# Probabilities times values by plain fp32 matmuls in a windowed attention block

## The chip, the cores and the metric

One core of a Trainium2 chip. The metric is the device time of one execution in microseconds. Engines are named as the profile names them: PE is TensorE (PEld its weight loads), DVE VectorE, ACT ScalarE, POOL GpSimd, SP SyncE, which here issues the transfers.

## The reference

Input x of 8 batches, 512 rows, 256 columns. Three blocks follow each other:

- x = x + 0.5 * FFN(layernorm(x)), where the FFN is another layernorm with gamma and beta, one 256 x 256 product with the weight quantized to -1, 0, 1, and a bias;
- x = x + attention(layernorm(x)): 16 query heads and 4 key/value heads of 128, rotary embedding on q and k, a causal window of 64 keys back, softmax, weights @ v, and an output projection Wo with bias;
- the first block once more.

The changed part is this line of it, with v repeated for the 4 query heads of a group:

```python
weights = jax.nn.softmax(scores, axis=-1)
out = jnp.einsum('bhqk,bhkd->bhqd', weights, v)
```

## The kernel before, in words

A batch's attention is cut into 16 units: 4 groups (one key/value head and its 4 query heads) times 4 blocks of 128 rows, and a block into 2 chunks of 64 queries. A chunk of 64 queries sees a window of 128 keys. So there are 128 units in the 8 batches. A unit passes through these steps:

- S, `scores` (L576): 4 plain fp32 matmuls of 128 columns, onto a mask that ScalarE wrote into the bank;
- VectorE's negated maxima (L747), ScalarE's exponentials with row sums (L913), VectorE's reciprocals (L753), GpSimd's scaling (L1023);
- T, `transpose_probs` (L622): 4 transposes into the bank probsT_p;
- probsT leaves the bank in two parts. ScalarE copies it to an fp32r tile, the high part (`probsT_high`, L945); VectorE subtracts that from the bank, the low part (`probsT_low`, L766);
- W, `values` (L607): for each of the 2 chunks the helper `three` (L567) does high x high, high x low, low x high as fp32r matmuls, values as weights, probsT as the 256 moving columns;
- `heads_high` (L938) and `heads_low` (L758) take the result out in two parts, and O, `project` (L593), multiplies them by Wo: 4 x 3 fp32r matmuls of 256 columns.

Beside the units stand jobs that share two banks in turn: K and Q (projections with rotary products by VectorE, L771, a swap of halves by two transfers, L538, a sum by GpSimd, L1030), V (values, 4 a batch; ScalarE's high part L968, VectorE's low part L792), and the FFN's and layernorms' transposes and products. A job waits in `wait_for_bank` (L629) until the job two before it has left its bank. For V that is the low part, by the semaphore v_lo. Odd chunks' windows start in the middle of a block, so values are also kept shifted by 64 rows in v_odd, filled by transfers from v_s (`shift_values`, L525): for each half batch 4 transfers, two for the high part and two for the low. W of the first unit of each half batch waits for them (L614).

The order of the work is written out by hand: one table a queue (TENSOR, VECTOR, SCALAR, GPSIMD, SYNC, L58 to L207), each with a prologue, a first, middle and last batch and an epilogue. In a name such as probsT14p the letter p, c or n says the previous, current or next batch. TensorE's order interleaves units and jobs, as "O7c W8c T9c S11c", so that a unit's evacuations run beside other matmuls. No other queue than its own orders a step; between queues semaphores do. In TensorE's prologue V00n stands ahead of K0n Q0n Q1n Q2n Q3n V01n. The values' low part has its place on VectorE behind pieces of weight splits (w3i, w5i).

Plain fp32 matmuls stand in S, in the transposes, in the opening product with beta (`beta_product`, L709, 256 columns) and in the two that open the score banks (`open_banks`, L718, 512 columns).

Of the kernel before, what the change touches and what calls it, by code (L numbers as in the profile page):

```python
# [37 lines left out]
P = 128  # L38
# [58 lines left out]
        w4i XT0n w3i XT1n w5i V00n K0n Q0n Q1n Q2n Q3n V01n  # L97
    """,
    "first": """
        K1c Q4c max0c Q5c max1c inv0c Q6c inv1c w11f probsT0c max2c V10c Q7c max3c  # L100
        inv2c heads0c K2c probsT1c Q8c heads1c max4c inv3c stats0n probsT2c Q9c stats1n inv4c heads2c
        max5c V11c probsT3c inv5c Q10c heads3c probsT4c max6c Q11c heads4c w12f inv6c probsT5c K3c
        max7c YT0n heads5c Q12c probsT6c inv7c max8c YT1n heads6c Q13c probsT7c FO0n max9c inv8c
        astats0n Q14c heads7c FO1n inv9c astats1n probsT8c Q15c max10c heads8c probsT9c XT0n inv10c max11c
        XT1n heads9c probsT10c inv11c max12c K0n heads10c inv12c Q0n probsT11c max13c heads11c V00n Q1n
        max14c inv13c probsT12c Q2n heads12c max15c inv14c probsT13c Q3n V01n inv15c
    """,
    "middle": """
        heads13p probsT14p K1c Q4c evac0p heads14p stats0p max0c max1c probsT15p inv0c Q5c inv1c V10c
        heads15p Q6c max2c probsT0c Q7c evac1p inv2c stats1p heads0c YT0p probsT1c K2c max3c Q8c  # L110
        heads1c stats0n YT1p inv3c probsT2c Q9c max4c FO0p heads2c Q10c max5c inv4c probsT3c V11c
        heads3c inv5c max6c probsT4c FO1p Q11c inv6c stats1n heads4c max7c probsT5c K3c YT0n max8c
        heads5c probsT6c Q12c inv7c YT1n heads6c Q13c max9c inv8c FO0n probsT7c astats0n inv9c Q14c
        FO1n astats1n heads7c probsT8c max10c XT0n Q15c heads8c max11c probsT9c inv10c XT1n heads9c inv11c
        probsT10c K0n max12c Q0n max13c heads10c probsT11c inv12c V00n Q1n heads11c max14c inv13c probsT12c
        Q2n inv14c heads12c max15c inv15c probsT13c Q3n V01n
    """,
    "last": """
        heads13p K1c Q4c probsT14p evac0p max0c stats0p max1c heads14p inv0c probsT15p Q5c V10c Q6c
        inv1c heads15p probsT0c max2c Q7c evac1p stats1p inv2c heads0c max3c YT0p probsT1c K2c Q8c  # L120
        heads1c YT1p probsT2c max4c inv3c Q9c heads2c FO0p max5c probsT3c Q10c inv4c V11c heads3c
        inv5c probsT4c max6c FO1p Q11c heads4c probsT5c inv6c K3c max7c inv7c heads5c Q12c probsT6c
        max8c Q13c heads6c inv8c probsT7c max9c Q14c heads7c max10c probsT8c inv9c Q15c inv10c heads8c
        max11c probsT9c inv11c heads9c max12c probsT10c heads10c inv12c max13c probsT11c heads11c max14c inv13c probsT12c
        heads12c max15c inv14c probsT13c inv15c
    """,
    "epilogue": """
        heads13p probsT14p heads14p probsT15p evac0p stats0p heads15p evac1p stats1p YT0p YT1p FO0p FO1p
# [127 lines left out]
def unit(x):  # L256
    return UNITS * x[2] + x[1]


def block_kernel(nc, x, wq, wk, wv, wo, ffn_wT, columns, rows, rope_tables, mask, ident, out):  # L260
# [3 lines left out]
    with ExitStack() as ctx:  # L264
# [23 lines left out]
        v_s = sb("v_s", [P, 2, BLOCKS, NKV * HD], F32R)  # L288
        v_odd = sb("v_odd", [P, 2, BLOCKS - 1, NKV * HD], F32R)

        probs = sb("probs", [P, 2, 4, P])
        probsT = sb("probsT", [P, 2, 2, GROUP * CHUNK], F32R)
# [844 lines left out]
```

## Time and profile before

| what | value |
|---|---|
| runs | 810.41, 810.8, 811.8 us, median 810.8 |
| the profiled execution | 812.07 us, span 810.2 us |
| mean granted TensorE clock | 0.994 |
| ScalarE, GpSimd busy | 515.1, 449.9 us |
| transfers | 70.53 MB |

The span runs from the first to the last profiled instruction; some 2 us lie around it. "Busy" counts a stretch once if instructions overlap. Ends of matmuls are modelled, so two of them overlap in a list, and a group's mean duration is not the distance between two of them: for that, start times are compared. A plain fp32 matmul shows as two records. "x6" merges six records of one kind, and "[0.24 <-DVE headsT L762]" is idle time ahead of it and what ended it.

### The profile page before, as it was taken

Reading aid. Unit: us, or ns where it says so; the run is one execution under the profiler, and the core shown is the slowest. Engines: PE = TensorE matmul, PEld = TensorE weight load, DVE = VectorE, ACT = ScalarE, POOL = GpSimd, SP = SyncE. Lnnn points to the kernel's source line nnn. Section 1 sums busy time; section 2 is a strip of 40 time slices with the busy share of each in tenths; the row PEclk is TensorE's granted clock in tenths of the full one; section 3 lists DMA queues with packets and bytes.
Section 4 is the critical chain, followed back from the end, with each engine's and each line's share of the span. In section 5 each row is a group of like instructions: output and inputs, shape, how many; then the busy total and the mean of one; then the engine's idle time right before and its main releaser. Section 6 shows DMA issues by size and latency. Waiting matters only on the chain.

```text
span 810.2 us, 16063 instructions
## 1 busy us (share of the span) xinstructions
PE 787.2 (97%) x5678; PEld 734.2 (91%) x5678; DVE 640.0 (79%) x1294; ACT 515.1 (64%) x1633; POOL 449.9 (56%) x435
## 2 busy tenths in 40 slices
PE   7899999999999999999999999999999999999984
PEld 6689999999999999999999999999999999999984
DVE  5888868888788877888779786888878887787644
ACT  5377765676657665676656766567666666574662
POOL 4577736575465644566446664556546564464532
PEclk9999999999999999999999999999999999999997
DMA  8464224442342424323234332444234242424300
GB/s 296 117 159 96 50 53 106 103 99 45 67 119 66 110 49 105 91 66 92 53 91 104 89 71 53 105 104 98 44 74 113 66 112 47 104 53 105 79 2 26
DMA packets 52431, 70.53 MB, mean 87 GB/s; under 512 B 7040, under 2 KB 30080, under 8 KB 52352
## 3 DMA queue, kind: packets, MB, share of 16 engines
q1 hardware_dynamic: 52064, 69.43, 35.2%
q8 instruction: 45, 0.74, 0.4%
q14 instruction: 34, 0.28, 0.1%
q10 hardware_dynamic: 288, 0.08, 0.0%
HBM read 10.76 MB, written 4.19 MB: 18 GB/s over the span
## 4 chain that ended last, share of the span: by engine, by line
PE 86%; DVE 5%; ACT 2%; issue 2%; POOL 2%; DMA 2%; SPq 0%; ACTq 0%; POOLq 0%
PE job_p L572 29%; PE attn_p L572 22%; PE scores_p L588 12%; PE heads_p L572 11%; PE probsT_p L626 6%; PE job_p L698 4%; PE job_p L687 2%; ACT headsT L942 1%; DVE headsT L762 1%; DMA q_s<-wk 1%; ACT probs L920 1%; DVE parts L842 1%; POOL q_s L1046 1%; DVE variance L851 1%; DMA rope_swap<-rope_sin 1%
## 5 line engine op out<-in xcount | busy, mean ns | idle before, releaser
L1026 POOL TENSOR_TENSOR probs<-probs,inv_sum 128x512 f32<-128x512 f32 x128 | 134.4, 1050 | 197.5 <-DVE inv_sum L756 197.3
L920 ACT ACTIVATE probs<-scores_p,neg_max 128x128 f32<-128x128 f32 x512 | 181.0, 372 | 52.4 <-DVE neg_max L750 51.8
L572 PE MATMUL attn_p<-wo_s,headsT 128*128 128x256 f32 x1536 | 208.9, 285 | 5.3 <-DVE headsT L762 5.3
L572 PE MATMUL job_p<-xnT,wq_s 128*128 128x512 f32 x768 | 204.9, 403 | 1.9 <-DVE v_s L794 1.8
L572 PEld LDWEIGHTS attn_p<-wo_s,headsT 128*128 128x128 f32 x1536 | 195.5, 191 | 11.7 <-DVE headsT L762 7.3
L1046 POOL TENSOR_TENSOR q_s<-rope_cos,rope_swap 128x512 f32<-128x512 f32 x128 | 164.4, 1292 | 54.4 <-DMA rope_swap<-rope_sin 54.3
L942 ACT ACTIVATE headsT<-heads_p,columns_s 128x512 fp32r<-128x512 f32 x128 | 88.2, 689 | 154.3 <-PE heads_p L572 152.8
L572 PEld LDWEIGHTS job_p<-xnT,wq_s 128*128 128x128 f32 x768 | 135.9, 189 | 26.9 <-DVE v_s L794 2.7
L762 DVE SCALAR_TENSOR_TENSOR headsT<-heads_p,columns_s,headsT 128x512 fp32r<-128x512 f32 x128 | 95.7, 748 | 59.6 <-ACT headsT L942 58.2
L588 PE MATMUL scores_p<-k_s,q_s 128*128 128x128 f32 x1024 | 135.2, 275 | 0.4 <-POOL q_s L1046 0.4
L588 PEld LDWEIGHTS scores_p<-k_s,q_s 128*128 128x128 f32 x1024 | 125.8, 192 | 2.5 <-POOL q_s L1046 0.9
L784 DVE SCALAR_TENSOR_TENSOR rope_sin<-job_p,columns_s,rope_t 128x512 f32<-128x512 f32 x160 | 119.0, 744 | 8.7 <-PE job_p L572 7.4
L789 DVE SCALAR_TENSOR_TENSOR rope_cos<-job_p,columns_s,rope_t 128x512 f32<-128x512 f32 x160 | 118.7, 742 | 0.0
L920 ACT ACTIVATION_READ_ACCUMULATOR probs<-scores_p,neg_max 128x1 f32 x512 | 108.1, 211 | 0.0
L750 DVE TENSOR_REDUCE neg_max<-scores_p 128x4 f32<-128x512 f32 x128 | 86.8, 682 | 16.6 <-PE scores_p L588 16.4
L768 DVE TENSOR_TENSOR probsT<-probsT_p,probsT 128x512 fp32r<-128x512 f32 x128 | 86.6, 677 | 4.4 <-ACT probsT L948 4.4
L948 ACT ACTIVATE probsT<-probsT_p 128x512 fp32r<-128x512 f32 x128 | 76.4, 597 | 20.8 <-PE probsT_p L626 20.7
L572 PE MATMUL heads_p<-probsT,v_s 128*128 128x256 f32 x480 | 79.0, 284 | 0.0
L935 ACT ACTIVATE scores_p<-mask_s 128x512 f32<-128x512 bf16 x128 | 77.6, 607 | 0.7
L626 PE MATMUL probsT_p<-identf,probs 128*128 128x128 f32 x512 | 77.0, 273 | 0.4 <-POOL probs L1026 0.2
L1046 POOL TENSOR_TENSOR k_s<-rope_cos,rope_swap 128x512 f32<-128x512 f32 x32 | 41.4, 1293 | 49.1 <-DMA rope_swap<-rope_sin 49.1
L572 PEld LDWEIGHTS heads_p<-probsT,v_s 128*128 128x128 f32 x480 | 66.7, 191 | 0.5 <-DVE probsT L768 0.4
(73 smaller groups left out, 925.3 us busy)
## 6 DMA issues: line engine op xcount, KB each, us to landing
rope_swap<-rope_sin SPq DMA_DIRECT2D x320, 128.0 KB, 2.3
v_odd<-v_s SPq DMA_DIRECT2D x64, 192.0 KB, 3.3
x_in<-x SPq DMA_DIRECT2D x16, 256.0 KB, 3.3
out<-x_res SPq DMA_DIRECT2D x16, 256.0 KB, 2.5
staging<-wo SPq DMA_DIRECT2D x2, 512.0 KB, 10.5
staging<-wq SPq DMA_DIRECT2D x2, 512.0 KB, 10.7
x_res<-wo SPq DMA_DIRECT2D x2, 512.0 KB, 3.8
x_res<-wv SPq DMA_DIRECT2D x1, 512.0 KB, 7.3
```

What stands on the lines that cost most here:

```text
L572: mm = nc.tensor.matmul(dst, a(p), b(q), start=first and clears and i == 0, stop=last and i == 2, skip_group_check=True)
L588: mm = nc.tensor.matmul(dst[:, 2 * cc + pair, :], q_s[g % 2][:, c, 2 * pair:2 * pair + 2, :], k_s[:, g % 2, w0:w0 + P], start=False, stop= ...
L626: mm = nc.tensor.transpose(probsT_p[:, k, :], probs[:, x[1] % 2, k, :], identf[:, :])
L750: nc.vector.tensor_reduce(neg_max[:, i, :], scores_p[i][:, :, :], AX.X, ALU.max, negate=True).then_inc(max_ready, 1)
L762: nc.vector.scalar_tensor_tensor(out=flat_heads(headsT[:, 1]), in0=flat_heads(heads_p[:, :]), scalar=bv_s[:, g:g + 1], in1=flat_heads(head ...
L768: nc.vector.tensor_tensor(probsT[:, 1, :, :], probsT_p[:, :, :].rearrange("p (c a) n -> p c (a n)", c=2), probsT[:, 0, :, :].bitcast(F32), ...
L784: nc.vector.scalar_tensor_tensor(out=rope_sin[:, r, :], in0=bank[:, :], scalar=bias, in1=sin_t, op0=ALU.add, op1=ALU.mult).then_inc(rope_s ...
L789: nc.vector.scalar_tensor_tensor(out=rope_cos[:, r, :], in0=bank[:, :], scalar=bias, in1=cos_t, op0=ALU.add, op1=ALU.mult).then_inc(rope_c ...
L920: ins = nc.scalar.activation(probs[:, i, k, :], scores_p[i][:, k, :], ACT.Exp, bias=neg_max[:, i, k:k + 1], accum_out=row_sum[:, i, k:k + 1])
L942: nc.scalar.activation(flat_heads(headsT[:, 0]), flat_heads(heads_p[:, :]), ACT.Identity, bias=bv_s[:, g:g + 1]).then_inc(heads_hi, 1)
L1026: nc.gpsimd.tensor_tensor(probs[:, i, :, :], probs[:, i, :, :], inv_sum[:, i, :].unsqueeze(2).to_broadcast([P, 4, P]), ALU.mult).then_inc( ...
L1046: nc.gpsimd.tensor_tensor(roped(x), as_roped(x, rope_cos[:, r, :]), as_roped(x, rope_swap[:, r, :]), ALU.add).then_inc(rope_added, 1)
```

## The change

`values` does one plain fp32 matmul a chunk in place of three fp32r ones. v_s, v_odd and probsT become fp32 and have one part, which ScalarE writes as it wrote the high part. `probsT_low` and `values_low` are gone, and their places in VectorE's tables (128 and 32 steps). Banks and tiles are released by ScalarE's semaphores probsT_taken and v_taken, and a half batch is shifted by two transfers. The other queues' orders stay. The diff, with the tables cut to samples:

```diff
--- before.py
+++ after.py
@@ -94,38 +94,38 @@
     "prologue": """
         ones0i stats0n stats1n tern0i beta0i YT0n YT1n FO0n astats0n FO1n astats1n w2i w1i w0i
-        w4i XT0n w3i XT1n w5i V00n K0n Q0n Q1n Q2n Q3n V01n
+        w4i XT0n w3i XT1n w5i K0n Q0n Q1n Q2n Q3n 
     """,
...
     "middle": """
-        heads13p probsT14p K1c Q4c evac0p heads14p stats0p max0c max1c probsT15p inv0c Q5c inv1c V10c
-        heads15p Q6c max2c probsT0c Q7c evac1p inv2c stats1p heads0c YT0p probsT1c K2c max3c Q8c
...
+        heads13p K1c Q4c evac0p heads14p stats0p max0c max1c inv0c Q5c inv1c 
+        heads15p Q6c max2c Q7c evac1p inv2c stats1p heads0c YT0p K2c max3c Q8c
...
@@ -285,11 +285,11 @@
         q_s = [sb(f"q_s{i}", [P, SEQ // CHUNK, GROUP, CHUNK]) for i in range(2)]
         k_s = sb("k_s", [P, 2, SEQ])
         w_full = k_s[:, 0, :].rearrange("p (c n) -> p c n", c=EC)
-        v_s = sb("v_s", [P, 2, BLOCKS, NKV * HD], F32R)
-        v_odd = sb("v_odd", [P, 2, BLOCKS - 1, NKV * HD], F32R)
+        v_s = sb("v_s", [P, BLOCKS, NKV * HD])
+        v_odd = sb("v_odd", [P, BLOCKS - 1, NKV * HD])
 
         probs = sb("probs", [P, 2, 4, P])
-        probsT = sb("probsT", [P, 2, 2, GROUP * CHUNK], F32R)
+        probsT = sb("probsT", [P, 2, GROUP * CHUNK])
         headsT = sb("headsT", [P, 2, GROUP, 2, CHUNK], F32R)
         neg_max = sb("neg_max", [P, 2, 4])
         row_sum = sb("row_sum", [P, 2, 4])
@@ -358,8 +358,7 @@
         inv_ready = sem("inv_ready")
         probs_ready = sem("probs_ready")
         probsT_ready = sem("probsT_ready")
-        probsT_hi = sem("probsT_hi")
-        probsT_lo = sem("probsT_lo")
+        probsT_taken = sem("probsT_taken")
         heads_ready = sem("heads_ready")
         heads_hi = sem("heads_hi")
         heads_lo = sem("heads_lo")
@@ -371,8 +370,7 @@
         rope_cosed = sem("rope_cosed")
         rope_swapped = [sem(f"rope_swapped{i}") for i in range(ROPES)]
         rope_added = sem("rope_added")
-        v_hi = sem("v_hi")
-        v_lo = sem("v_lo")
+        v_taken = sem("v_taken")
         ln_hi = sem("ln_hi")
         ln_lo = sem("ln_lo")
         xn_hi = sem("xn_hi")
@@ -479,10 +477,10 @@
 
             return ("XT" if x[0][0] == "a" else "YT" + x[0][-1], *x[1:])
 
-        def v_part(i, s):
+        def v_part(i):
             half, m = i
             width = NKV * HD // 2
-            return v_s[:, s, 2 * m:2 * m + 2, half * width:(half + 1) * width]
+            return v_s[:, 2 * m:2 * m + 2, half * width:(half + 1) * width]
 
         def flat_heads(ap):
             return ap.rearrange("p h c q -> p (h c q)")
@@ -527,13 +525,10 @@
                 _, half, b = x
 
 
-                sp.wait_ge(v_lo, VALUES["V", (half, 1), b] + 1)
+                sp.wait_ge(v_taken, VALUES["V", (half, 1), b] + 1)
                 cols = slice(half * NKV * HD // 2, (half + 1) * NKV * HD // 2)
-                for s in range(2):
-                    sp.dma_start(v_odd[0:CHUNK, s, :, cols].bitcast(F32),
-                                 v_s[CHUNK:P, s, 0:BLOCKS - 1, cols].bitcast(F32)).then_inc(v_shifted, 16)
-                    sp.dma_start(v_odd[CHUNK:P, s, :, cols].bitcast(F32),
-                                 v_s[0:CHUNK, s, 1:BLOCKS, cols].bitcast(F32)).then_inc(v_shifted, 16)
+                sp.dma_start(v_odd[0:CHUNK, :, cols], v_s[CHUNK:P, 0:BLOCKS - 1, cols]).then_inc(v_shifted, 16)
+                sp.dma_start(v_odd[CHUNK:P, :, cols], v_s[0:CHUNK, 1:BLOCKS, cols]).then_inc(v_shifted, 16)
 
             def swap_halves(x):
 
@@ -608,15 +603,15 @@
                 u, (g, t), b = unit(x), divmod(x[1], BLOCKS), x[2]
 
 
-                pe.wait_ge(probsT_lo, u + 1)
+                pe.wait_ge(probsT_taken, u + 1)
                 if x[1] in (0, UNITS // 2):
 
-                    pe.wait_ge(v_shifted, 64 * (SHIFTED["shift", x[1] // (UNITS // 2), b] + 1))
+                    pe.wait_ge(v_shifted, 32 * (SHIFTED["shift", x[1] // (UNITS // 2), b] + 1))
                 for cc in range(2):
                     c = 2 * t + cc
                     src, at = (v_s, max(c - 1, 0) // 2) if c == 0 or c % 2 else (v_odd, c // 2 - 1)
-                    mm = three(heads_p[:, :, cc, :], lambda s: src[:, s, at, g * HD:(g + 1) * HD],
-                               lambda s: probsT[:, s, cc, :], True, True, cc == 0)
+                    mm = nc.tensor.matmul(heads_p[:, :, cc, :], src[:, at, g * HD:(g + 1) * HD], probsT[:, cc, :],
+                                          start=cc == 0, stop=True, skip_group_check=True)
                 mm.then_inc(heads_ready, 1)
 
             def transpose_probs(x):
@@ -634,7 +629,7 @@
                 if was[0] in ("Q", "K"):
                     pe.wait_ge(rope_cosed, ROPED[was] + 1)
                 elif was[0] == "V":
-                    pe.wait_ge(v_lo, VALUES[was] + 1)
+                    pe.wait_ge(v_taken, VALUES[was] + 1)
                 elif was[0] == "XT":
                     pe.wait_ge(xn_lo, XN[was] + 1)
                 elif was in FFN_IN:
@@ -763,11 +758,6 @@
                     out=flat_heads(headsT[:, 1]), in0=flat_heads(heads_p[:, :]), scalar=bv_s[:, g:g + 1],
                     in1=flat_heads(headsT[:, 0]).bitcast(F32), op0=ALU.add, op1=ALU.subtract).then_inc(heads_lo, 1)
 
-            def probsT_low(x):
-                dve.wait_ge(probsT_hi, unit(x) + 1)
-                nc.vector.tensor_tensor(probsT[:, 1, :, :], probsT_p[:, :, :].rearrange("p (c a) n -> p c (a n)", c=2),
-                                        probsT[:, 0, :, :].bitcast(F32), ALU.subtract).then_inc(probsT_lo, 1)
-
             def rope_products(x):
 
                 kind, i, b = x
@@ -788,11 +778,6 @@
                     dve.wait_ge(rope_added, n + 1 - ROPES)
                 nc.vector.scalar_tensor_tensor(out=rope_cos[:, r, :], in0=bank[:, :], scalar=bias, in1=cos_t,
                                                op0=ALU.add, op1=ALU.mult).then_inc(rope_cosed, 1)
-
-            def values_low(x):
-                dve.wait_ge(v_hi, VALUES[x] + 1)
-                nc.vector.tensor_tensor(v_part(x[1], 1), bank_of(x)[:, :].rearrange("p (k n) -> p k n", k=2),
-                                        v_part(x[1], 0).bitcast(F32), ALU.subtract).then_inc(v_lo, 1)
 
             def xn_low(x):
                 dve.wait_ge(xn_hi, XN[x] + 1)
@@ -891,8 +876,8 @@
                                                op0=ALU.mult, op1=ALU.add).then_inc(bias_ready, 1)
 
             for x in DVE_STEPS:
-                {"max": max_of, "inv": invert_sums, "heads": heads_low, "probsT": probsT_low,
-                 "K": rope_products, "Q": rope_products, "V": values_low, "XT": xn_low,
+                {"max": max_of, "inv": invert_sums, "heads": heads_low,
+                 "K": rope_products, "Q": rope_products, "XT": xn_low,
                  "YT1": ffn_in_low, "YT2": ffn_in_low, "FO1": ffn_out, "FO2": ffn_out,
                  "stats1": statistics, "stats2": statistics, "astats": statistics,
                  "evac": after_attention, "w": split_low, "ones": set_ones, "tern": ternary, "beta": fold_beta}[x[0]](x)
@@ -942,11 +927,11 @@
                 nc.scalar.activation(flat_heads(headsT[:, 0]), flat_heads(heads_p[:, :]), ACT.Identity,
                                      bias=bv_s[:, g:g + 1]).then_inc(heads_hi, 1)
 
-            def probsT_high(x):
+            def take_probsT(x):
 
                 act.wait_ge(probsT_ready, unit(x) + 1)
-                nc.scalar.activation(probsT[:, 0, :, :], probsT_p[:, :, :].rearrange("p (c a) n -> p c (a n)", c=2),
-                                     ACT.Copy).then_inc(probsT_hi, 1)
+                nc.scalar.activation(probsT[:, :, :], probsT_p[:, :, :].rearrange("p (c a) n -> p c (a n)", c=2),
+                                     ACT.Copy).then_inc(probsT_taken, 1)
 
             def normalize(x):
 
@@ -971,8 +956,8 @@
                 if b:
 
                     act.wait_ge(heads_ready, UNITS * (b - 1) + (UNITS if half else UNITS // 2))
-                nc.scalar.activation(v_part(x[1], 0), bank_of(x)[:, :].rearrange("p (k n) -> p k n", k=2),
-                                     ACT.Copy).then_inc(v_hi, 1)
+                nc.scalar.activation(v_part(x[1]), bank_of(x)[:, :].rearrange("p (k n) -> p k n", k=2),
+                                     ACT.Copy).then_inc(v_taken, 1)
 
             def xn_high(x):
                 act.wait_ge(job_ready, JOBS[x] + 1)
@@ -995,7 +980,7 @@
             act.wait_ge(power_ready, 1)
             nc.scalar.activation(thr[:, 3:4], minus_half[:, 0:1], ACT.Copy)
             for x in ACT_STEPS:
-                {"exp": exp_of, "mask": mask_bank, "heads": heads_high, "probsT": probsT_high,
+                {"exp": exp_of, "mask": mask_bank, "heads": heads_high, "probsT": take_probsT,
                  "norm1": normalize, "norm2": normalize, "anorm": normalize, "V": values_high, "XT": xn_high,
                  "YT1": ffn_in_high, "YT2": ffn_in_high, "w": split_high, "abs": sum_magnitudes}[x[0]](x)
```

## Rows read from the trace of the kernel before

**Rows 1.** The page, part 1: busy us (share of the span) xinstructions

```profile
PE 787.2 (97%) x5678; PEld 734.2 (91%) x5678; DVE 640.0 (79%) x1294; ACT 515.1 (64%) x1633; POOL 449.9 (56%) x435
```

**Rows 2.** Stretches: start:end length, busy us (x) of PE PEld DVE ACT POOL, clock, DMA

```profile
0.00:50.00 50.00, 40.46 (x217) 32.74 (x218) 37.50 (x74) 24.62 (x59) 27.71 (x29) 1.00 0.68 200
50.00:768.00 718.00, 716.72 (x5246) 673.63 (x5245) 582.94 (x1179) 469.73 (x1511) 408.51 (x394) 1.00 0.35 84
768.00:810.20 42.20, 30.02 (x218) 27.81 (x218) 19.61 (x44) 20.77 (x65) 13.64 (x14) 0.89 0.04 13
```

**Rows 3.** PE's waits, one row each of 50 to 768, 0 to 50, 768 on

```profile
PE attn_p L572 <- DVE headsT L762: 0.5, 2, 0.2
...
PE job_p L572 <- DVE v_s L794: 1.8, 1, 1.8
...
PE attn_p L572 <- DVE headsT L762: 5.0, 8, 1.6
```

**Rows 4.** Groups of instructions: shapes xcount | busy us, mean ns | idle before, releasers

```profile
L572 PE MATMUL heads_p<-probsT,v_s 128*128 128x256 f32 x480 | 79.0, 284 | 0.0
...
L572 PE MATMUL heads_p<-probsT,v_odd 128*128 128x256 f32 x288 | 50.3, 283 | 0.0
...
L572 PEld LDWEIGHTS heads_p<-probsT,v_s 128*128 128x128 f32 x480 | 66.7, 191 | 0.5 <-DVE probsT L768 0.4
...
L768 DVE TENSOR_TENSOR probsT<-probsT_p,probsT 128x512 fp32r<-128x512 f32 x128 | 86.6, 677 | 4.4 <-ACT probsT L948 4.4
...
L948 ACT ACTIVATE probsT<-probsT_p 128x512 fp32r<-128x512 f32 x128 | 76.4, 597 | 20.8 <-PE probsT_p L626 20.7
```

**Rows 5.** Timeline, PE, mid span: start us, us, what, xcount (merged)

```profile
405.28 0.88 PE L572 MATMUL heads_p<-probsT,v_s 128*128 128x256 f32 x6
406.00 0.60 PE L626 MATMUL probsT_p<-identf,probs 128*128 128x128 f32 x4
406.44 1.06 PE L588 MATMUL scores_p<-k_s,q_s 128*128 128x128 f32 x8
407.25 1.64 PE L572 MATMUL job_p<-xnT,wq_s 128*128 128x512 f32 x6
408.72 1.60 PE L572 MATMUL job_p<-wv_s,xnT 128*128 128x256 f32 x12
```

**Rows 6.** Timeline, PE, opening: transposes, beta product, opening of the score banks

```profile
7.73 1.11 PE L687 MATMUL job_p<-identf,y 128*128 128x128 f32 x4
8.64 1.06 PE L730 MATMUL heads_p<-identf 128*128 128x128 f32 x4
...
10.13 1.49 PE L714 MATMUL attn_p<-w_tern,columns_s 128*128 128x256 f32 x3
11.41 0.42 PE L687 MATMUL job_p<-identf,y 128*128 128x128 f32 x1
...
15.61 1.88 PE L723 MATMUL scores_p<-identf 128*128 128x512 f32 x4
17.32 1.05 PE L730 MATMUL heads_p<-identf 128*128 128x128 f32 x8
```

**Rows 7.** Timeline, all engines, 23 to 41 us: values and rotary sums

```profile
23.78 0.59 ACT L974 ACTIVATE v_s<-job_p 128x512 fp32r<-128x512 f32 x1
...
27.09 0.68 DVE L794 TENSOR_TENSOR v_s<-job_p,v_s 128x512 fp32r<-128x512 f32 x1
...
27.82 6.21 PE L572 MATMUL job_p<-xnT,wq_s 128*128 128x512 f32 x24 [1.76 <-DVE v_s L794]
...
36.41 3.80 POOL L1046 TENSOR_TENSOR q_s<-rope_cos,rope_swap 128x512 f32<-128x512 f32 x3 [1.87 <-DMA rope_swap<-rope_sin]
```

**Rows 8.** Timeline, PE, ending: one turn of the loop

```profile
781.41 0.88 PE L572 MATMUL heads_p<-probsT,v_s 128*128 128x256 f32 x6
...
783.86 1.70 PE L572 MATMUL attn_p<-wo_s,headsT 128*128 128x256 f32 x12 [0.24 <-DVE headsT L762]
...
785.39 0.52 PE L572 MATMUL heads_p<-probsT,v_odd 128*128 128x256 f32 x3
```

More of the change, by code:

```diff
@@ L103 @@
[L103 to L106, printed above, removed]
+        K1c Q4c max0c Q5c max1c inv0c Q6c inv1c w11f max2c Q7c max3c
+        inv2c heads0c K2c Q8c heads1c max4c inv3c stats0n Q9c stats1n inv4c heads2c
@@ L107 @@
+        max5c inv5c Q10c heads3c max6c Q11c heads4c w12f inv6c K3c
+        max7c YT0n heads5c Q12c inv7c max8c YT1n heads6c Q13c FO0n max9c inv8c
+        astats0n Q14c heads7c FO1n inv9c astats1n Q15c max10c heads8c XT0n inv10c max11c
+        XT1n heads9c inv11c max12c K0n heads10c inv12c Q0n max13c heads11c Q1n
+        max14c inv13c Q2n heads12c max15c inv14c Q3n inv15c
     """,
     "middle": """
-        heads13p probsT14p K1c Q4c evac0p heads14p stats0p max0c max1c probsT15p inv0c Q5c inv1c V10c
@@ L110 @@
-        heads15p Q6c max2c probsT0c Q7c evac1p inv2c stats1p heads0c YT0p probsT1c K2c max3c Q8c
[L111 to L114, printed above, removed]
@@ L115 @@
-        probsT10c K0n max12c Q0n max13c heads10c probsT11c inv12c V00n Q1n heads11c max14c inv13c probsT12c
-        Q2n inv14c heads12c max15c inv15c probsT13c Q3n V01n
+        heads13p K1c Q4c evac0p heads14p stats0p max0c max1c inv0c Q5c inv1c
+        heads15p Q6c max2c Q7c evac1p inv2c stats1p heads0c YT0p K2c max3c Q8c
+        heads1c stats0n YT1p inv3c Q9c max4c FO0p heads2c Q10c max5c inv4c
+        heads3c inv5c max6c FO1p Q11c inv6c stats1n heads4c max7c K3c YT0n max8c
+        heads5c Q12c inv7c YT1n heads6c Q13c max9c inv8c FO0n astats0n inv9c Q14c
@@ L117 @@
+        FO1n astats1n heads7c max10c XT0n Q15c heads8c max11c inv10c XT1n heads9c inv11c
+        K0n max12c Q0n max13c heads10c inv12c Q1n heads11c max14c inv13c
+        Q2n inv14c heads12c max15c inv15c Q3n
     """,
     "last": """
-        heads13p K1c Q4c probsT14p evac0p max0c stats0p max1c heads14p inv0c probsT15p Q5c V10c Q6c
-        inv1c heads15p probsT0c max2c Q7c evac1p stats1p inv2c heads0c max3c YT0p probsT1c K2c Q8c
-        heads1c YT1p probsT2c max4c inv3c Q9c heads2c FO0p max5c probsT3c Q10c inv4c V11c heads3c
@@ L122 @@
[L122 to L125, printed above, removed]
+        heads13p K1c Q4c evac0p max0c stats0p max1c heads14p inv0c Q5c Q6c
+        inv1c heads15p max2c Q7c evac1p stats1p inv2c heads0c max3c YT0p K2c Q8c
@@ L126 @@
+        heads1c YT1p max4c inv3c Q9c heads2c FO0p max5c Q10c inv4c heads3c
+        inv5c max6c FO1p Q11c heads4c inv6c K3c max7c inv7c heads5c Q12c
+        max8c Q13c heads6c inv8c max9c Q14c heads7c max10c inv9c Q15c inv10c heads8c
+        max11c inv11c heads9c max12c heads10c inv12c max13c heads11c max14c inv13c
+        heads12c max15c inv14c inv15c
     """,
     "epilogue": """
-        heads13p probsT14p heads14p probsT15p evac0p stats0p heads15p evac1p stats1p YT0p YT1p FO0p FO1p
+        heads13p heads14p evac0p stats0p heads15p evac1p stats1p YT0p YT1p FO0p FO1p
```

3 lines of the change are left out of this document (removed).

## The prediction

> **What bounds the kernel now.** I read the busy shares first. TensorE's matmuls are busy for 787.2 of 810.2 us, VectorE for 640.0, ScalarE for 515.1 [rows 1]. An average can hide stages, so the table of three stretches comes next [rows 2]: between 50 and 768 us matmuls are busy for 716.72 of 718.00 us, while VectorE has 135 us free. Before 50 us TensorE is busy for 40.46 of 50 us, behind 768 us for 30.02 of 42.20 us. Third, TensorE's own waits: in the 718 us the largest one, for headsT from VectorE, is 0.5 us in total; the opening has one of 1.8 us on VectorE's low part of the values; the ending has 5.0 us on headsT [rows 3]. So for 718 us the time is the sum of TensorE's own instructions. A removed VectorE instruction is worth nothing there, and a changed matmul is worth its full change. Only the two ends are chains of latencies.
>
> **Pace, not duration.** A matmul's listed duration (284 ns for heads_p [rows 4]) overlaps its neighbours', so I take paces from start times [rows 5]. Six matmuls of a unit's values start at 405.28 and the next step at 406.00: 0.72 us, 120 ns for one 256-column fp32r matmul. The scores are plain fp32 already: 512 matmuls leave 1024 records, two for one. Eight records of 128 columns start at 406.44, the next step at 407.25. That is 101 ns for each of eight, or 116 ns if the first matmul of the next step is only listed early and seven gaps make up the time. I take 112 ns, nearer the upper end, because the next step, the query projection, does look stretched: 1.47 us for six fp32r matmuls of 512 columns, 245 ns each, over twice 120. A transpose of 128 columns, also plain fp32, paces at 110 ns (0.44 us for four).
>
> **Part 1: values by plain fp32.** For each of 128 units two products of 256 columns replace 3 x 2 fp32r matmuls. Two records each makes four. What does one cost at 256 columns? The trace has three neighbours [rows 6]. At 512 columns, the four records that open the score banks start at 15.61 and the next step at 17.32: 427.5 ns each. At 128 columns it is 112 ns. A line through both gives 217.5 ns at 256. The third has the very shape: the product with beta, three records from 10.13 to 11.41, 427 ns each. But that is in the opening, where four transposes take 0.91 us (7.73 to 8.64) against 0.44 us later, so TensorE was at its 1.2 GHz level there although the granted clock is listed as 1.00 for the stretch. Halved, 213.5 ns. I take 216 ns, between them, with ends 213 and 218. A unit then takes 4 x 0.216 = 0.864 us in place of 0.72, 0.144 more, and **128 units 18.4 us more** (0.132 x 128 = 16.9 at the low end, 0.152 x 128 = 19.5 at the high end). Nothing hides it: in the middle TensorE has no idle time to give, and in the ending the values stand in the chain. There values start at 781.41, the projection waits for their evacuation until 783.86, and the next values start at 785.39 [rows 8], a loop of 3.98 us that holds the whole product once, so it too grows by 0.144 us a unit. Weight loads fall from six to four per unit; I credit them with nothing, because they run beside the matmuls.
>
> That the four records cost more than the six is the row's statement. The Trainium skill (FP8 and Floating Point Precision, TensorE Precision Notes) says that true fp32 takes four passes through the array. The paces agree in kind: two records of two passes each. They do not agree if every pass is charged at fp32r's 120 ns; that is a rival below.
>
> **Part 2: VectorE's low parts go.** 128 of probsT at 677 ns (86.6 us [rows 4]) and 32 of the values at 0.68 us (the one at 27.09 [rows 7]), 21.8 us. VectorE falls to about 532 us. In the middle this is worth at most the waits that exist: 0.5 us on headsT and some tenths on others. I take 0.5 us, ends 0 and 1.1 (718.00 less 716.72 with the rounding off). The probabilities become ready one VectorE step earlier, and no unit of the middle waits for them. Everything behind the removed steps on VectorE's queue (maxima, head low parts, rotary products) comes no later. Nothing new becomes late.
>
> **Part 3: releases by ScalarE.** The copies of probsT and values stay, one each, with an fp32 target where it was fp32r. No row has a copy to fp32. The nearest is the copy of probsT as it is, 597 ns [rows 4]; I take that. It could be somewhat shorter or as long as the 677 ns of VectorE's step beside it; both ends are covered, since that step of 677 ns no longer stands behind it on the way to TensorE. A bank of values is free after ScalarE's copy. This shows once: in the prologue ScalarE's copy starts at 23.78, the low part sits behind weight splits on VectorE until 27.09, and the query projection starts at 27.82 after a wait [rows 3, 7]. With the bank free at about 24.4 it can start when the key projection ends, at about 25.8: 1.9 us sooner. But the next three projections wait for rotary products on VectorE, which move up only by the 0.68 us removed there and a few tenths of better overlap; behind them come the swap transfers and GpSimd's sums, three in a row from 36.41 to 40.21, on which the first scores wait. So of 1.9 us **I take 1.1 us** as reaching the first scores, ends 0 (if the swap transfers land when they do now, next to the weight loads) and 1.9.
>
> **Part 4: the shift transfers.** Two in place of four for each half batch, half the bytes. SP's queue gets shorter ahead of the swaps of rotary products. No TensorE wait in the middle names them; credited at nothing. They can only make transfers earlier.
>
> **Sum.** +18.4 - 0.5 - 1.1 = **+16.8 us**. The profiled execution took 812.07 us around its span of 810.2; with the change 828.9. The median of the runs shown is 810.8, 1.3 below that execution, so the forecast is 827.6 us. Bounds: 16.9 - 1.1 - 1.9 = +13.9 (824.7) and +19.5 (830.3); with 1 to 2 us on each side for the seams between fp32r and fp32 steps and for the measurement, 823 to 832.
>
> **Rivals.**
> *Weight loads set the pace (ends faster).* TensorE's weight loads are busy for 91% of the span, and for values one takes 191 ns, longer than the 120 ns pace of its matmul [rows 1, 4, 5]. If each load, and not its columns, costs 120 ns, four loads take 0.48 us, 0.24 us less per unit: -30.7 us, and with the 1.6 us of gains 778.5. It decides if one record of 256 fp32 columns paces below 180 ns, the break-even 0.72/4. Against it: fp32 records pace at 112 with 128 columns and at 427.5 with 512 [rows 5, 6]; columns set it, not loads. Chance 0.03. The Trainium skill (Perfetto Trace Analysis, Identifying the Most-Contended Engine) would have TensorE judged by the busy share of weight loads and not by that of matmuls; by that, fewer loads should help, and the rows here speak against it.
>
> *Four passes at fp32r's pace.* If a pass costs what an fp32r matmul costs, a unit takes 8 x 120 = 0.96 us, 0.24 more: +30.7 - 1.6, 839.9 us. Against it: at 512 columns four passes take 2 x 427.5 = 855 ns, 214 a pass, under the 245 of one fp32r matmul [rows 5, 6]. Chance 0.04.
>
> *VectorE was what held TensorE.* If hidden delays by VectorE (79% busy) are in the middle's paces, 108 us less on it could pay for the matmuls. All idle time of TensorE in the span is 23.0 us [rows 1]; to break even 80% of it would have to vanish, and 12.2 us of it lie in the ending behind latencies that the change leaves alone. Even half of it gives 18.4 - 11.5, 817.7 us. Chance of 818 to 823: 0.04; of no change or better by it 0.02.
>
> *The change doesn't do what it says* (fp32 tiles still multiplied in one pass). Two matmuls of 120 ns a unit would show; -61 us. The scores' double records speak against. Chance 0.01.
>
> **How the numbers follow.** Forecast with its bounds: 0.86. A measurement of this kernel can tell about 0.2%, 1.6 us. Faster by more: 0.03 + 0.01 + 0.01 = 0.05; within: 0.01; slower: 0.94. The range 823 to 832 leaves out the rivals, 0.14 in all.
>
> **What the changed profile would show.** 512 records of heads_p with 256 columns where 768 stood; four of them and then the next step after 0.86 us (right) or 0.48 or 0.96 (rivals). Batches of the middle 2.3 us longer, 16 x 0.144. VectorE near 532 us busy. The wait on v_s gone and the first scores near 39.2 us. The ending's loop at 4.12 us for 3.98. I am wrong if the middle doesn't grow by some 16 us, or if a new wait of TensorE of more than 1 us stands in it.

## The result, and the profile after

The changed kernel takes **825.93 us** (median of 4 runs, 825.58 to 826.44), the kernel before 811.12 us beside it; the ratio is 1.0183, 95% interval 1.0166 to 1.0201. It is slower by 14.8 us, where +16.8 was forecast. The profiled execution took 826.44 us around a span of 824.6 us, 14.4 us more than the span of before.

The busy shares of the page, to be read against [rows 1]:

```profile
PE 803.1 (97%) x5422; PEld 733.7 (89%) x5422; DVE 547.3 (66%) x1134; ACT 516.0 (63%) x1633; POOL 448.9 (54%) x435
```

VectorE is 92.7 us less busy and TensorE 15.9 us more. (The removed VectorE steps summed to 108.4 us; busy time counts overlapping neighbours once, so it falls by less.) The stretches, against [rows 2], with the same columns:

```profile
0.00:50.00 50.00, 41.28 (x216) 34.24 (x217) 35.77 (x70) 25.09 (x61) 27.63 (x29) 1.00 0.65 192
50.00:780.00 730.00, 730.00 (x4993) 671.19 (x4992) 495.26 (x1026) 468.71 (x1506) 406.01 (x392) 1.00 0.32 74
780.00:824.60 44.60, 31.84 (x217) 28.27 (x215) 16.29 (x38) 22.25 (x67) 15.26 (x15) 0.96 0.06 18
```

For 730 us matmuls leave no gap that the profile shows. VectorE has 235 us free there, and no use for them. The groups of the changed instructions, against [rows 4] (out<-in shapes xcount | busy us, mean ns | idle before):

```profile
L613 PE MATMUL heads_p<-probsT,v_s 128*128 128x256 f32 x320 | 89.9, 378 | 0.0
...
L613 PE MATMUL heads_p<-probsT,v_odd 128*128 128x256 f32 x192 | 57.2, 379 | 0.0
```

320 and 192 make the 512 records, for 768. What they cost is in TensorE's timeline of the middle, against [rows 5]:

```profile
411.95 1.03 PE L613 MATMUL heads_p<-probsT,v_s 128*128 128x256 f32 x4
412.82 0.60 PE L621 MATMUL probsT_p<-identf,probs 128*128 128x128 f32 x4
413.25 1.06 PE L583 MATMUL scores_p<-k_s,q_s 128*128 128x128 f32 x8
414.07 1.63 PE L567 MATMUL job_p<-xnT,wq_s 128*128 128x512 f32 x6
```

Four records from 411.95 to 412.82 take 0.87 us (another unit: 406.93 to 407.80). In the five batches from 205 to 700 us a unit ahead of transposes takes 0.86 or 0.87 us, in the mean 0.866, so the forecast 0.864 holds. The steps beside it have kept their length: 0.43 or 0.44 us for the transposes, 0.82 or 0.81 for the scores.

A whole batch of the middle can be read off the chain of waits, where one merged piece of 18 matmuls returns once a batch. Before (start us, us, what):

```profile
203.54 2.81 PE job_p L572 x18
...
300.01 2.81 PE job_p L572 x18
...
396.31 2.82 PE job_p L572 x18
...
492.67 2.82 PE job_p L572 x18
...
588.65 2.82 PE job_p L572 x18
```

and after:

```profile
206.63 2.81 PE job_p L567 x18
...
304.75 2.81 PE job_p L567 x18
...
402.85 2.81 PE job_p L567 x18
...
500.97 2.81 PE job_p L567 x18
...
599.09 2.81 PE job_p L567 x18
```

Before, the batches take 96.47, 96.30, 96.36 and 95.98 us; after, 98.12, 98.10, 98.12 and 98.12. They have become longer, and even. Sixteen units at +0.145 would be +2.3; against the uneven batches of before only 1.6 to 2.1 shows. Something of 0.2 to 0.7 us a batch came back, though the largest wait of TensorE in that stretch of before was 0.5 us in all [rows 3].

The opening and the ending come from TensorE's waits (engine line waited for: us in total, times, longest; the first line is of 0 to 50 us, the second of 780 us on). The wait of 1.8 us on the values' low part [rows 3] is gone, and one of 1.1 us for a rotary product stands in its place; the ending's waits are as long as before:

```profile
PE job_p L567 <- DVE rope_cos L779: 1.1, 1, 1.1
...
PE attn_p L567 <- DVE headsT L757: 5.0, 8, 1.6
```

TensorE's timeline of the opening (the key projection, the query projections, the first scores), before and after; the query projections of before are in [rows 7]:

```profile
24.43 1.63 PE L572 MATMUL job_p<-xnT,wk_s 128*128 128x512 f32 x6 [0.69 <-DVE xnT L799]
...
40.27 2.05 PE L588 MATMUL scores_p<-k_s,q_s 128*128 128x128 f32 x16
```

```profile
25.32 1.61 PE L567 MATMUL job_p<-xnT,wk_s 128*128 128x512 f32 x6 [0.70 <-DVE xnT L784]
26.77 1.52 PE L567 MATMUL job_p<-xnT,wq_s 128*128 128x512 f32 x6
29.43 4.82 PE L567 MATMUL job_p<-xnT,wq_s 128*128 128x512 f32 x18 [1.14 <-DVE rope_cos L779]
...
40.40 1.95 PE L583 MATMUL scores_p<-k_s,q_s 128*128 128x128 f32 x16
```

and of the ending, against [rows 8]:

```profile
794.17 1.69 PE L567 MATMUL attn_p<-wo_s,headsT 128*128 128x256 f32 x12 [0.24 <-DVE headsT L757]
...
798.30 1.69 PE L567 MATMUL attn_p<-wo_s,headsT 128*128 128x256 f32 x12 [0.24 <-DVE headsT L757]
```

The first query projection now follows the key projection at 26.77; the next ones wait for rotary products, as foreseen. From the first key projection to the first scores it is 15.08 us (25.32 to 40.40). Before it was 15.84 us (24.43, the key projection, to 40.27). The scores' absolute time is no measure: in this execution the key projection itself starts 0.89 us later. The identity and the first part of x landed earlier than before, but the second part of x later (the statistics that wait for it start at 7.27 us, before at 6.62), and the FFN product behind it ends later. The changed steps have no part in that. The ending's loop takes 4.13 us, 794.17 to 798.30, for 3.98.

### The profile page after: what moved, and what is told of

Same layout as the page of the kernel before. It is cut to its first block, busy times and chain, and to the rows that moved or that the text cites. A ratio compares the mean times of both kernels' runs of the same rounds, so it can differ in the third digit from the quotient of the medians.

```text
span 824.6 us, 15359 instructions
## 1 busy us (share of the span) xinstructions
PE 803.1 (97%) x5422; PEld 733.7 (89%) x5422; DVE 547.3 (66%) x1134; ACT 516.0 (63%) x1633; POOL 448.9 (54%) x435
## 4 chain that ended last, share of the span: by engine, by line
PE 93%; DVE 3%; issue 1%; POOL 1%; ACT 1%; DMA 1%; SPq 0%; ACTq 0%; POOLq 0%
PE job_p L567 31%; PE attn_p L567 23%; PE heads_p L613 13%; PE scores_p L583 13%; PE probsT_p L621 6%; PE job_p L693 4%; PE job_p L682 2%; DVE headsT L757 1%; ACT headsT L927 1%; DMA x_in<-x 1%; POOL q_s L1031 1%; DVE parts L827 0%; DVE wq_s L740 0%; POOL wo_s L994 0%; PE attn_p L709 0%
## 5 line engine op out<-in xcount | busy, mean ns | idle before, releaser
L933 ACT ACTIVATE probsT<-probsT_p 128x512 f32<-128x512 f32 x128 | 76.3, 596 | 22.1 <-PE probsT_p L621 22.0
L613 PE MATMUL heads_p<-probsT,v_s 128*128 128x256 f32 x320 | 89.9, 378 | 0.0
L621 PEld LDWEIGHTS probsT_p<-identf,probs 128*128 128x128 f32 x512 | 63.3, 140 | 12.7 <-POOL probs L1011 0.5
L613 PEld LDWEIGHTS heads_p<-probsT,v_s 128*128 128x128 f32 x320 | 58.2, 189 | 7.2
```

Source lines behind the costliest of these rows:

```text
L613: mm = nc.tensor.matmul(heads_p[:, :, cc, :], src[:, at, g * HD:(g + 1) * HD], probsT[:, cc, :], start=cc == 0, stop=True, skip_group_chec ...
L621: mm = nc.tensor.transpose(probsT_p[:, k, :], probs[:, x[1] % 2, k, :], identf[:, :])
```

## The experiments

Two theories stood for the 4.1 us that came back (128 x 0.145 = 18.5 less the span's 14.4): VectorE's lighter queue, or the longer matmuls themselves, which cover small waits. A third, that the execution profiled before was an unlucky one, is taken up in the account further down. The first four kernels take the change apart.

**The matmuls alone.**

```diff
-                    mm = three(heads_p[:, :, cc, :], lambda s: src[:, s, at, g * HD:(g + 1) * HD],
-                               lambda s: probsT[:, s, cc, :], True, True, cc == 0)
+                    mm = nc.tensor.matmul(heads_p[:, :, cc, :], src[:, 0, at, g * HD:(g + 1) * HD].bitcast(F32),
+                                          probsT[:, 0, cc, :].bitcast(F32),
+                                          start=cc == 0, stop=True, skip_group_check=True)
```

> The kernel before with the matmuls of the values alone changed: plain fp32, on the high parts of values and probabilities; all of VectorE's low parts, their waits and transfers stay (the low parts are computed and not used, so the output lacks them). Pace theory: a unit's values take 0.865 us for 0.72, so 128 units cost 18.5 us. The changed kernel's span grew by only 14.4, so 4.1 us came back. If lighter VectorE queues gave them back, nothing comes back here: about 811.1 + 18.5 = 829.6 us. If the longer matmuls themselves cover small waits of TensorE in the middle (0.15 us at each batch's first key projection and some of 0.3 to 0.6), 3 us of it come back here too: about 826.5 us.

Measured: 827.65 us (826.97 to 828.26), ratio 1.0203, interval 1.0189 to 1.0217; before beside it 811.04. That is +16.6, between the two theories: 1.9 of the 18.5 came back with all of VectorE's work in place. Its batches, in the chain of waits:

```profile
305.61 2.81 PE job_p L572 x18
...
501.90 2.81 PE job_p L572 x18
...
600.37 2.81 PE job_p L572 x18
```

Two batches take 196.29 us, 98.15 each, and the third 98.47: near the whole change's 98.12, not quite as even. Its opening is that of before, 24.98 to 40.85, 15.87 us.

**No low parts, the matmuls as before.** From VectorE's tables all probsT and V steps go, a half batch is shifted by two transfers in place of four (the wait for v_shifted with them), and:

```diff
-                pe.wait_ge(probsT_lo, u + 1)
+                pe.wait_ge(probsT_hi, u + 1)
-                    mm = three(heads_p[:, :, cc, :], lambda s: src[:, s, at, g * HD:(g + 1) * HD],
-                               lambda s: probsT[:, s, cc, :], True, True, cc == 0)
+                    mm = three(heads_p[:, :, cc, :], lambda s: src[:, 0, at, g * HD:(g + 1) * HD],
+                               lambda s: probsT[:, 0, cc, :], True, True, cc == 0)
-                    pe.wait_ge(v_lo, VALUES[was] + 1)
+                    pe.wait_ge(v_hi, VALUES[was] + 1)
```

> The kernel before with three fp32r matmuls a chunk, but without VectorE's low parts of probabilities and values, the banks and tiles released by ScalarE, two shift transfers for four. All three matmuls read the high parts, so the low parts are left out of the result; TensorE's instructions are as many and as long as before. If the lighter VectorE gave the 4.1 us back: about 807 us. If the longer matmuls covered the waits: only the opening's 0.8 us, about 810.3 us.

Measured: 808.86 us, ratio 0.997 (0.996 to 0.9981), -2.2 us, again between the two theories. Taking 160 instructions, 108 us of work, from VectorE is worth 2.2 us. The parts add up: +16.6 - 2.2 = +14.4, the whole change +14.8. The opening is 24.92 to 40.03, 15.11 us. The batches:

```profile
298.67 2.82 PE job_p L565 x18
...
490.61 2.82 PE job_p L565 x18
...
586.57 2.82 PE job_p L565 x18
```

Two batches take 191.94 us, 95.97 each, and the third 95.96. So 95.97 is the batch with fp32r matmuls when no irregular wait is left, and the 96.30 to 96.47 of before held 0.3 to 0.5 us of such waits. But 98.12 less 95.97 is 2.15, not 2.32. One wait of 0.15 a batch is left in the kernel without low parts and absent after. It is at the key projection for the next batch. First before, then after:

```profile
291.33 0.52 PE L572 MATMUL heads_p<-probsT,v_odd 128*128 128x256 f32 x3
291.36 0.69 DVE L799 TENSOR_TENSOR xnT<-job_p,xnT 128x512 fp32r<-128x512 f32 x1 [0.31 <-ACT xnT L979]
...
291.69 0.52 PE L572 MATMUL heads_p<-probsT,v_s 128*128 128x256 f32 x3
...
292.19 1.17 PE L572 MATMUL job_p<-xnT,wk_s 128*128 128x512 f32 x4
```

```profile
295.93 0.60 PE L613 MATMUL heads_p<-probsT,v_odd 128*128 128x256 f32 x2
295.95 0.69 DVE L784 TENSOR_TENSOR xnT<-job_p,xnT 128x512 fp32r<-128x512 f32 x1 [0.31 <-ACT xnT L964]
...
296.36 0.59 PE L613 MATMUL heads_p<-probsT,v_s 128*128 128x256 f32 x2
...
296.79 1.40 PE L567 MATMUL job_p<-xnT,wk_s 128*128 128x512 f32 x5
```

Both take 0.86 us from the values' start to the projection's. Before, 0.72 of it was matmuls and 0.14 a wait for VectorE's low part of xnT, which ended at 292.05. After, the longer product fills the same 0.86: this unit's extra 0.145 costs nothing. So it is in all five batches from 205 to 700 us (before, the projection starts 0.50 or 0.51 us after the first of the values' last three matmuls, whose pace makes 0.36), and the kernel without low parts has the same 0.51 us (290.34 to 290.85). It stands in each batch but the last, which has no next one to project for: 7 x 0.145 = 1.0 us that the longer matmuls, and not the removed low parts, give back. Matmuls are listed 0.16 us longer than their pace (0.52 us from 291.69, where three paces are 0.36), so a wait shorter than that shows as no idle time at all.

**One half of the low parts each.** In the first only the probsT steps go, in the second only the V steps, with their waits and transfers (the diffs are the halves of the one above).

> As the run without low parts, but the values' low parts on VectorE and their release of the bank stay; only the 128 low parts of the transposed probabilities go (left out of the result). If VectorE's load is what made the waits of the middle: 128 x 0.68 us is 80% of what was removed, so most of the middle's 3 us come here, 808 us; the wait of 1.8 us in the opening on the values' low part is still there. Rival, that these waits come from elsewhere: 811.1 us, no change.

> As the run without low parts, but the 128 low parts of the transposed probabilities stay on VectorE; only the 32 of the values go (left out of the result), with the early release of their banks and half of the shift transfers. Opening theory: the query projection starts 1.9 us sooner and the first scores some 0.8 us sooner, and the middle keeps its waits: 810.3 us. Rival, that the shift transfers and the values' banks made the middle's waits: 807 to 808 us.

Measured: 811.75 us for the first, ratio 1.0 (0.9991 to 1.0009); 809.78 us for the second, 0.9984 (0.9975 to 0.9993). By the medians four fifths of what VectorE was relieved of is worth nothing by itself, to within 0.7 us; the 32 steps of the values are worth 1.3 us of the 2.2. The first's profiled execution has an opening of 17.33 us (24.38 to 41.71), because TensorE's granted clock was 0.65 from 28 to 30 us and 0.50, its 1.2 GHz level, from 30 to 32; whether its other executions had that too isn't known. Its middle does not depend on it, and that is no shorter either (726.34 us from the first scores to the first long wait of the ending, beside 726.41 in the kernel under the next heading, where no low part is gone). The second's opening is 15.09 us (25.24 to 40.33), so some 0.75 us of its 1.3 is the first values' bank.

**The opening alone.**

```diff
-        w4i XT0n w3i XT1n w5i V00n K0n Q0n Q1n Q2n Q3n V01n
+        w4i XT0n w3i XT1n V00n w5i K0n Q0n Q1n Q2n Q3n V01n
```

> The kernel before with one step moved in VectorE's prologue: the low part of the first values ahead of the last weight split (w5i) instead of behind it, everything computed. It takes the wait of 1.8 us at the first query projection away without any other change. Theory: the first scores start some 0.8 us earlier and the middle keeps its waits, about 810.3 us. Rival, the opening is bound by the swap transfers and GpSimd's sums alone: no change, 811.1 us.

Measured: 809.98 us, before beside it 811.78, ratio 0.9981 (0.9972 to 0.999). One step moved in one table gives as much as the removal of 32. The key projection, the first query projection and the first scores:

```profile
24.44 1.63 PE L572 MATMUL job_p<-xnT,wk_s 128*128 128x512 f32 x6 [0.70 <-DVE xnT L799]
...
25.91 1.53 PE L572 MATMUL job_p<-xnT,wq_s 128*128 128x512 f32 x6
...
39.54 1.95 PE L588 MATMUL scores_p<-k_s,q_s 128*128 128x128 f32 x16
```

15.10 us, 0.74 less than before; the rest of the 1.8 us between the medians is no more than their spread (809.35 to 811.34 against 809.93 to 812.88). Its chain of waits shows something else, four batches of the middle, with the matmuls and all of VectorE's steps there as before:

```profile
202.65 2.82 PE job_p L572 x18
...
586.68 2.82 PE job_p L572 x18
```

They take 384.03 us, where the execution of before took 385.11 (203.54 to 588.65) and the kernel without low parts would take 383.87 at its pace. So most of the irregular waits of the profiled execution of before are absent here, with nothing changed in the middle. Neither half of the change is needed for that. Put onto the kernel with the matmuls alone changed, the same line:

> The run with the matmuls alone changed, and the low part of the first values ahead of w5i. The matmuls alone gave 827.65 us, the whole change 825.93. If the rest of 1.7 us is the opening's: about 826.2 us. If it is VectorE's lighter load in the middle, which this kernel doesn't have: 827.6 us. The low parts are computed and not used, as there.

Measured: 826.53 us (825.93 to 827.35), ratio 1.0187 (1.0173 to 1.0201), 1.1 below the matmuls alone and 0.6 above the whole change. The opening is again 15.10 us (24.72 to 39.82). So of the 1.7 us between those two the opening is 0.77; the early release as a whole gives 1.1 by the medians, and the last 0.6 is within the spread of either.

**Does the load or the column set the pace?** The changed kernel with twice the loads for the same columns:

```diff
-                    mm = nc.tensor.matmul(heads_p[:, :, cc, :], src[:, at, g * HD:(g + 1) * HD], probsT[:, cc, :],
-                                          start=cc == 0, stop=True, skip_group_check=True)
+                    for two_heads in (slice(0, 2), slice(2, 4)):
+                        mm = nc.tensor.matmul(heads_p[:, two_heads, cc, :], src[:, at, g * HD:(g + 1) * HD],
+                                              probsT[:, cc, CHUNK * two_heads.start:CHUNK * two_heads.stop],
+                                              start=cc == 0 and two_heads.start == 0, stop=True,
+                                              skip_group_check=True)
```

> The changed kernel with each plain fp32 product of 256 columns cut into two of 128: the same columns, twice the weight loads and records (eight for four), the result complete. If columns set the pace: 8 x 0.112 = 0.90 us a unit for 0.865, at most 4 us more, about 830 us. If weight loads or instructions set it, a record would keep its 0.216 us: 1.73 us a unit, 110 us more, about 936 us.

and the kernel before with each fp32r product cut the same way, twelve matmuls of 128 columns for six of 256:

> The kernel before with each fp32r product of 256 columns cut into two of 128, twelve matmuls a unit for six, the result complete. This measures what an fp32r matmul costs in itself, where fp32 pays 108 ns a pass of 256 columns and fp32r 120 ns. If fp32r streams a column at the rate of one fp32 pass and its 120 ns are columns alone, twelve take 0.72 to 0.75 us: up to 4 us more, 811 to 815 us. If its matmuls have a floor near 120 ns (a weight load or a start), twelve take 1.44 us: 92 us more, about 903 us. If an fp32r matmul of few columns runs at plain fp32's four passes, twelve take 12 x 0.22 = 2.6 us: about 1055 us.

Measured: 828.61 us (ratio 1.0207, 1.0191 to 1.0224) for plain fp32, and 884.55 us (1.0898, 1.0883 to 1.0913) for fp32r. The timelines of a unit, first fp32, then fp32r:

```profile
412.41 1.06 PE L614 MATMUL heads_p<-probsT,v_s 128*128 128x128 f32 x8
413.30 0.60 PE L624 MATMUL probsT_p<-identf,probs 128*128 128x128 f32 x4
```

```profile
433.59 0.78 PE L572 MATMUL heads_p<-probsT,v_odd 128*128 128x128 f32 x6
434.21 0.84 PE L572 MATMUL heads_p<-probsT,v_s 128*128 128x128 f32 x6
434.88 0.62 PE L628 MATMUL probsT_p<-identf,probs 128*128 128x128 f32 x4
```

Eight fp32 records take 0.89 us, 111 ns each, against 0.865 for four of twice the columns: columns set plain fp32's pace. Twelve fp32r matmuls take 1.29 us, 107.5 ns each, against 0.72 for six of 256 columns at 120. Halving the columns saved 12 ns of 120. So at 128 columns something other than the columns holds an fp32r matmul near 107 ns, and at 256 it runs little above that. I call it a floor; fewer columns than 128 were not measured. Whether it is the weight load or the start of a matmul isn't separated by this kernel.

**A version faster than both.** Everything is computed as in the kernel before; V00n moves ahead as in the last move, w5i takes the place of w3i, and the weight split w3i, 2.5 us of VectorE ahead of the first rotary products, goes to GpSimd:

```diff
 VECTOR
-        w4i XT0n w3i XT1n w5i V00n K0n Q0n Q1n Q2n Q3n V01n
+        w4i XT0n w5i XT1n V00n K0n Q0n Q1n Q2n Q3n V01n
 GPSIMD
-        scale0n scale1n half0i bias0n bias1n ascale0n ascale1n w6i w8i K0n Q0n Q1n Q2n Q3n
+        scale0n scale1n half0i bias0n bias1n ascale0n ascale1n w6i w8i w3i K0n Q0n Q1n Q2n Q3n
```

> The kernel before with fp32r matmuls and all low parts, everything computed, and three moves in the prologue: the low part of the first values ahead of the weight split w5i on VectorE, w5i in the place of w3i, and w3i (2.5 us on VectorE, needed only by the second key projection) on GpSimd, which idles for some 4 us there. If the opening is bound by VectorE's queue: its rotary products start 1.5 us sooner than with the first move alone (809.98 us), so about 808.5 to 809.0 us. If it is bound by swap transfers and GpSimd's sums: as with the first move alone, 810 us; if w3i delays GpSimd's sums, 811 us or more.

Measured: 809.11 us, before beside it 811.16, ratio 0.9975 (0.9966 to 0.9984), 0.25% faster than before.

```profile
24.81 1.63 PE L572 MATMUL job_p<-xnT,wk_s 128*128 128x512 f32 x6 [0.69 <-DVE xnT L799]
26.27 6.50 PE L572 MATMUL job_p<-xnT,wq_s 128*128 128x512 f32 x24
26.70 1.83 POOL L1009 TENSOR_TENSOR wk_s<-q_s,wk_s 128x768 fp32r<-128x768 f32 x1
...
35.12 3.79 POOL L1046 TENSOR_TENSOR q_s<-rope_cos,rope_swap 128x512 f32<-128x512 f32 x3 [2.25 <-DMA rope_swap<-rope_sin]
...
38.96 2.05 PE L588 MATMUL scores_p<-k_s,q_s 128*128 128x128 f32 x16
```

Four query projections run as one piece and the first scores come after 14.15 us, 1.7 less than before and 0.95 less than with the first move alone. Of the 1.5 us expected beyond the first move, 0.95 came in the opening. In the whole time they are not clear of noise: this kernel lies 2.05 us below its neighbour of before, the first move 1.8. GpSimd now waits 2.25 us for the swap transfers, which stand where VectorE's queue stood.

## Why the prediction was right

**The bound and the main term held.** TensorE's own instructions are the time of the middle; the records cost 0.865 us a unit, forecast 0.864 with ends of 0.852 and 0.872, and so 18.5 us in place of 18.4. The line between 128 and 512 columns and the halved row of the opening were both near, and their middle was right.

**The opening** was given 1.1 us and gave 0.75, alike in the six kernels that release the first values early by one step (15.08 to 15.11 us from key projection to scores, for 15.81 to 15.87 in three that don't; the fourth is the one at a lower clock). The first scores, forecast near 39.2, came at 40.40 with that and the 0.89 us by which the key projection was late. The query projection did start 1.9 us sooner after it, and the chain behind it was the one named: rotary products, swap transfers, GpSimd's sums. Of the step sizes in it little more than the 0.68 us removed from VectorE's queue came through; the "few tenths of better overlap" were under 0.1.

**The term that was mis-sized is the middle's waits**, "I take 0.5 us, ends 0 and 1.1". The step that failed was to take the idle time of a TensorE with modelled ends (718.00 less 716.72) as the most that could come back. A wait under 0.16 us does not show there. The sentence "Nothing hides it" went wrong with it: at seven key projections the longer product is hidden behind such a wait. The prediction's own sign of being wrong, a middle that "doesn't grow by some 16 us", did come about. The middle grew by 13.7 us.

The whole account of the spans is cut at the first scores and at the first long wait of the ending. Up to the first scores it is +0.1 us (40.27 to 40.40): the key projection 0.89 later, the stretch behind it 0.76 shorter. The middle is +13.7, where 121 units at 0.145 would be +17.5. The seven turns of the ending's loop add 1.0, as they should. The stretch behind them is 0.5 shorter, 13.92 for 14.39 us. That is no work of the change. Both have a wait of 3.95 us there, with two FFN products behind it. Before, the granted clock fell to 0.50, the 1.2 GHz level, during that wait, and the four transposes behind it are listed with 1.08 us. After, it fell within the first product, and they are listed with 0.63. The kernel with the first values early has 0.63 and 13.97 us too. So of the span's 4.1 us 3.8 came back in the middle, 0.76 in the opening and 0.5 by the clock at the very end, less 0.9 for the late transfer. The middles of the kernels, the two with halved matmuls left out:

| kernel | first scores | first long wait of the ending | between |
|---|---|---|---|
| before | 40.27 | 767.93 | 727.66 |
| first values early | 39.54 | 765.95 | 726.41 |
| probsT's low parts gone | 41.71 | 768.05 | 726.34 |
| values' low parts gone | 40.33 | 766.71 | 726.38 |
| w3i on GpSimd | 38.96 | 765.18 | 726.22 |
| no low parts | 40.03 | 765.19 | 725.16 |
| the whole change | 40.40 | 781.78 | 741.38 |
| the matmuls alone | 40.85 | 783.09 | 742.24 |
| the matmuls alone, first values early | 39.82 | 782.14 | 742.32 |

Of the 3.8 us, 1.25 (727.66 to 726.41) vanish in the kernel with the first values early, whose middle has the same instructions. The earlier start is hardly the reason: with plain fp32 the middle is no shorter by it (742.24 and 742.32). So I put the 1.25 down to the one execution of before that was profiled, which was among the slower ones, 812.07 us for a median of 811.12. A second trace of the same kernel, which would show it, was not kept. Another 1.25 go with all of VectorE's low parts (726.41 to 725.16), and 0.9 in the same comparison with plain fp32 (742.32 to 741.38). These are single executions. By the medians the first step is 1.1 us (0.4 if each is taken against its neighbour of before), the second 0.6. So relief of VectorE is worth 1 us or so in the middle, and that is not clear of noise. The last 1.3 us (17.5 less 741.38 - 725.16) are given back by the longer matmuls with VectorE relieved, and 1.0 of it is the key projection's wait. Where the irregular waits come from (single batches have them and others not) stays open.

By the medians, which average over such executions, 18.5 less 14.8 or 3.7 us came back where 1.6 was forecast: 0.75 in the opening, 1.0 at the key projections, and some 2 us of small waits of which no experiment here gives the shares. The forecast erred by 0.35 us too much in the opening and by some 2.5 us too little in the middle. The result lies 1.7 us under the forecast and inside the range, because the main term was right. Part of that is luck: with the main term as measured, 18.5, both other terms at their ends (1.1 and 1.9) leave +15.5, and +14.8 is under that. The range holds it by the low end of the main term (16.9) and the margin.

**The copies** to fp32 by ScalarE take 596 ns, for 597 to fp32r, as assumed.

**The rivals.** Weight loads setting the pace is excluded for plain fp32 (twice the loads, 828.61 for 825.93 us, and not 936). The Trainium skill (Perfetto Trace Analysis, Identifying the Most-Contended Engine) has TensorE's distance to its limit judged by the arithmetic done as a share of the peak and by the busy share of weight loads, not by the busy share of matmuls. Here the weight loads' share fell from 91 to 89% while TensorE stayed without a gap for 730 us, so it did not tell what fewer loads are worth. The rival is nearer for fp32r, which at 256 columns runs only 12 ns above its pace at 128. Four passes at fp32r's pace is excluded by the 0.865 us, for 0.96. The trace shows two records a matmul and no passes. By the four passes that the Trainium skill states (FP8 and Floating Point Precision, TensorE Precision Notes), a pass of 256 columns would take an estimated 108 ns, half of a record's 216, against 120 for one fp32r matmul. That VectorE's load could pay for the matmuls is excluded by the kernel without its low parts, -2.2 us for 108 us of work.

## What to carry to other kernels

Three fp32r products of 256 columns (0.72 us for two chunks) cost less on TensorE than one plain fp32 product (0.865 us), by 17%. The exchange can only pay where the engine that makes the low parts is the bound, and here it was not. Relief for an engine that is 79% busy can be worth almost nothing (2.2 us for 108); look at which of its steps stands ahead of the bound engine at the start and the end, and move that one first. When counting what waits could come back, measure a repeated piece of the schedule from start to start, not the idle column, and in more than one execution: two traces whose middles have the same instructions differed by 1.25 us here.

## What the runs showed of the hardware

An fp32r matmul with 128 moving columns paced at 107.5 ns, with 256 at 120 and with 512 at 227 to 246, by the steps beside it (1.36 to 1.48 us for six query projections in the middle of the kernel before). A plain fp32 record paced at 111, 216 and 427.5 ns for the same columns. So cutting an fp32r product from 256 to 128 columns saves next to nothing, while a plain fp32 record of 128 columns costs hardly more than an fp32r matmul of 128: there three fp32r products (0.32 us) would be dearer than one plain fp32 product of two records (0.22 us). The order of the two forms turns between 128 and 256 columns.
